# The layernorm statistics tail of an attention stage, moved behind the next slab's scores and shifted from VectorE to ScalarE

## The chip, the cores and the metric

One Trainium2 chip, 8 cores, each with its own 4096 tokens; no communication between them. The metric is the device time in microseconds of the slowest core. Engines: TensorE (PE), VectorE (DVE), ScalarE (ACT), GpSimd (POOL), SyncE (SP).

## The reference

Local attention over three neighbours, then a mixture of eight experts, each followed by a residual and a layernorm without weights:

```python
def _layernorm(x, axis=-1, eps=1e-5):
    m = jnp.mean(x, axis=axis, keepdims=True)
    v = jnp.var(x, axis=axis, keepdims=True)
    return (x - m) / jnp.sqrt(v + eps)
# x: (4, 8192, 1024), 16 heads of 64
xp = x @ Wp.T + bp
q = (xp @ Wq.T + bq) * scale; k = xp @ Wk.T + bk; v = xp @ Wv.T + bv
attn = softmax over the tokens s-1, s, s+1 of q . k
x = _layernorm(x + (attn-weighted v) @ Wo.T + bo)
# top 2 of 8 experts by sigmoid router, square(relu(x @ W1)) @ W2
x = _layernorm(x + ffn(x))
```

## The kernel before

All tensors of the attention stage are feature-major: 128 features on the partitions, 8 chunks of them (`dc`), 512 tokens along the free axis. A slab is 512 tokens; a core has 8 slabs. The weights Wp and Wq, Wk, Wv are multiplied together first. The feed-forward stage follows after a barrier of all engines (L691 to L699); it reads the normalised slabs back from HBM.

The order of the work is written out by hand: each `seg_` function appends instructions to the lists of the five engines, and every engine runs its own list strictly in order. The loop at L672 emits for each slab s:

1. `seg_scores(s)`: 24 products q times k on DVE into six slots (`pslots`, three per chunk), 32 matmuls on PE that sum them by head into `ps_s0` and `ps_s2`
2. `seg_softmax_a(s)`: two exponentials on ACT (L454, L456), their sum on DVE (L459)
3. `seg_ln1_tail(s-1)`: PE broadcasts the inverse deviation and the scaled mean from `stb` to 128 partitions (L623, L627), ACT copies both out of PSUM (L638, L640), DVE normalises the 8 chunks with 16 instructions, SP stores the slab
4. `seg_softmax_b(s)`: Ln and Exp on ACT (L466, L468), two weight products on DVE
5. `seg_qkv(s+1)`: 384 matmuls in 48 groups over two banks, each evicted by ACT (L407)
6. `seg_wsum(s)`, `seg_wo(s)`: weighted sum of v, output projection (64 matmuls), residual on DVE
7. `seg_ln1_stats_mm(s)`: sums and sums of squares over the features, by matmuls with a column of ones into `ps_s1` and `ps_st`, with the squares from DVE
8. `seg_xt(s+2)`: four x tiles and a halo of two tokens, loaded by POOL one after the other, transposed by PE (L340, L364), copied by ACT (L348, L372)
9. `seg_ln1_stats_tail(s)`: on one partition of 512 tokens, DVE scales sum and sum of squares, squares the mean and subtracts (L594 to L600), ACT does Ln and Exp for the inverse deviation (L605, L607), DVE multiplies it by the mean and casts both to bf16 in `stb` (L610 to L614)

Ahead of the loop stand `seg_xt(0)`, `seg_qkv(0)`, `seg_xt(1)`. The slabs 6 and 7 have no item 8, slab 7 has no item 5, and after the loop `seg_ln1_tail(7)` remains. A `drain` is put between two instructions of one engine that touch the same tensor.

Of the kernel before, what the change touches and what calls it, by code (L numbers as in the profile page):

```python
# [9 lines left out]
AF = mybir.ActivationFunctionType  # L10
# [3 lines left out]
D = 1024  # L14
# [80 lines left out]
def _h(ap):  # L95
    return ap.tensor if hasattr(ap, "tensor") else ap


def build_program(T):
    assert T % SLAB == 0  # L100
    NSLAB = T // SLAB
# [37 lines left out]
    s_pe = semh("s_pe")  # L139
    s_dve = semh("s_dve")  # L140
    s_act = semh("s_act")
# [3 lines left out]
    p = _Prog(block)  # L145
# [64 lines left out]
    for xi, (wxt_h, c_sb, cb_sb, scale) in enumerate(  # L210
# [4 lines left out]
        for dc in range(NCH):  # L215
            for jg in range(2):
# [3 lines left out]
                for kc in range(NCH):  # L220
# [5 lines left out]
                             inc=(s_pe if kc == NCH - 1 else None))  # L226
# [5 lines left out]
                          reads=[_h(role.t)], writes=[_h(c_sb)], inc=s_act)  # L232
                role.consumed(s_act, va)
        for jc in range(NCH):
            psfb.wait_writer(p)
            p.wait("tensor", s_ld, base_ld)
            for kc in range(NCH):
# [5 lines left out]
                         inc=(s_pe if kc == NCH - 1 else None))  # L243
# [5 lines left out]
                      reads=[_h(psfb.t)], writes=[_h(cb_sb)], inc=s_dve)  # L249
            psfb.consumed(s_dve, va)  # L250
        if xi < 2:
# [32 lines left out]
    stn = psb("stn", [1, 3 * 512], F32)  # L284
    stb = psb("stb", [1, 1024], BF16)
# [5 lines left out]
    ps_s = [_PsumRole(pst("ps_s0", [128, 512], F32)),  # L291
            _PsumRole(pst("ps_s1", [128, 512], F32)),
            _PsumRole(pst("ps_s2", [128, 512], F32))]
    ps_st = _PsumRole(pst("ps_st", [128, 512], F32))
# [7 lines left out]
    sn = lambda i: stn[:, i * 512:(i + 1) * 512]  # L302
# [10 lines left out]
    g_lnact = 0  # L313
# [6 lines left out]
    SS = {}  # L320
# [129 lines left out]
    def seg_softmax_a(s):  # L450
        p.wait("scalar", s_pe, SS[("scores", s)])
        p.wait("scalar", s_act, g_exp)
        p.wait("scalar", s_pe, g_mb)
        p.do("scalar", lambda En: En.activation(sm(0), ps_s[0].t[0:NH, :], AF.Exp),  # L454
             reads=[_h(ps_s[0].t)], writes=[_h(smt)], inc=s_act)
        v_e = p.do("scalar", lambda En: En.activation(sm(1), ps_s[2].t[0:NH, :], AF.Exp),  # L456
                   reads=[_h(ps_s[2].t)], writes=[_h(smt)], inc=s_act)
        p.wait("vector", s_act, v_e)
        v_sm = p.do("vector", lambda En: En.scalar_tensor_tensor(sm(2), sm(0), 1.0, sm(1), ALU.add, ALU.add),  # L459
                    reads=[_h(smt)], writes=[_h(smt)], inc=s_dve)  # L460
        SS[("v_sm", s)] = v_sm
        return v_e
# [125 lines left out]
        SS[("v2s", s)] = v2s  # L588

    def seg_ln1_stats_tail(s):  # L590
        p.wait("vector", s_pe, SS[("v2s", s)])
        p.wait("vector", s_act, g_lnact)
        p.wait("vector", s_pe, SS.get("v_mb", 0))
        p.do("vector", lambda En: En.tensor_scalar_mul(sn(0), ps_s[1].t[0:1, :], 1.0 / D),  # L594
             reads=[_h(ps_s[1].t)], writes=[_h(stn)], inc=s_dve)
        p.do("vector", lambda En: En.tensor_scalar_mul(sn(1), ps_st.t[0:1, :], 1.0 / D),
             reads=[_h(ps_st.t)], writes=[_h(stn)], inc=s_dve)
        p.do("vector", lambda En: En.tensor_mul(sn(2), sn(0), sn(0)),
             reads=[_h(stn)], writes=[_h(stn)], inc=s_dve)
        v_var = p.do("vector", lambda En: En.tensor_sub(sn(1), sn(1), sn(2)),  # L600
                     reads=[_h(stn)], writes=[_h(stn)], inc=s_dve)
        ps_s[1].consumed(s_dve, v_var)
        ps_st.consumed(s_dve, v_var)
        p.wait("scalar", s_dve, v_var)
        p.do("scalar", lambda En: En.activation(sn(2), sn(1), AF.Ln, bias=LN_EPS),  # L605
             reads=[_h(stn)], writes=[_h(stn)], inc=s_act)
        v_rs = p.do("scalar", lambda En: En.activation(sn(1), sn(2), AF.Exp, scale=-0.5),  # L607
                    reads=[_h(stn)], writes=[_h(stn)], inc=s_act)
        p.wait("vector", s_act, v_rs)
        p.do("vector", lambda En: En.tensor_mul(sn(2), sn(0), sn(1)),  # L610
             reads=[_h(stn)], writes=[_h(stn)], inc=s_dve)
        p.do("vector", lambda En: En.tensor_copy(stb[:, 0:512], sn(1)),
             reads=[_h(stn)], writes=[_h(stb)], inc=s_dve)
        v_stb = p.do("vector", lambda En: En.tensor_copy(stb[:, 512:1024], sn(2)),  # L614
                     reads=[_h(stn)], writes=[_h(stb)], inc=s_dve)
        SS[("v_stb", s)] = v_stb
        return v_rs

    def seg_ln1_tail(s):
        par = s % 2  # L620
        p.wait("tensor", s_dve, SS[("v_stb", s)])
        ps_s[1].wait_writer(p)
        p.do("tensor", lambda En: En.matmul(ps_s[1].t[:], onescol[0:1, :],  # L623
                                            stb[0:1, 0:512], start=True, stop=True),
             inc=s_pe)
        ps_st.wait_writer(p)
        v_mb = p.do("tensor", lambda En: En.matmul(ps_st.t[:], onescol[0:1, :],  # L627
                                                   stb[0:1, 512:1024], start=True, stop=True),
                    inc=s_pe)
        SS["v_mb"] = v_mb  # L630
        p.wait("scalar", s_pe, v_mb)
        sbp = pslots[2]
        mbp = pslots[3]
        for sl in (2, 3):
            if pslot_guard[sl] is not None:
                p.wait("scalar", *pslot_guard[sl])
                pslot_guard[sl] = None
        p.do("scalar", lambda En: En.copy(sbp, ps_s[1].t[:]),  # L638
             reads=[_h(ps_s[1].t)], writes=[pslot_t[2]], inc=s_act)
        v_bb = p.do("scalar", lambda En: En.copy(mbp, ps_st.t[:]),  # L640
                    reads=[_h(ps_st.t)], writes=[pslot_t[3]], inc=s_act)
        ps_s[1].consumed(s_act, v_bb)
        ps_st.consumed(s_act, v_bb)
        pslot_guard[2] = (s_act, v_bb)
        pslot_guard[3] = (s_act, v_bb)
        p.wait("vector", s_act, v_bb)
        if rstg_free[par] is not None:
            p.wait("vector", *rstg_free[par])
        for dc in range(NCH):
            t0n = pslots[dc % 2]  # L650
            p.do("vector", lambda En, o=t0n, r=r1c(s, dc):
                 En.tensor_mul(o, r, sbp),
                 reads=[_h(q_sb), pslot_t[2]], writes=[pslot_t[dc % 2]], inc=s_dve)
            p.do("vector",
                 lambda En, o=r1n_stg[:, par * NCH * SLAB + dc * SLAB: par * NCH * SLAB + (dc + 1) * SLAB],
                 a=t0n:
                 En.tensor_sub(o, a, mbp),
                 reads=[pslot_t[dc % 2], pslot_t[3]], writes=[_h(r1n_stg)], inc=s_dve)
        g_r1n[par] = s_dve.n
        p.wait("sync", s_hw, s_hw.n)  # L660
        p.wait("sync", s_dve, s_dve.n)
        p.do("sync",
             lambda En, o=r1n_hbm.rearrange("p (c t) -> p c t", t=T)[:, :, s * SLAB:(s + 1) * SLAB],
             i_=r1n_stg[:, par * NCH * SLAB:(par + 1) * NCH * SLAB].rearrange("p (c t) -> p c t", t=SLAB):
             En.dma_start(out=o, in_=i_),
             inc=s_hw, inc_by=16)
        rstg_free[par] = (s_hw, s_hw.n)
# [4 lines left out]
    for s in range(NSLAB):  # L672
        seg_scores(s)
        v_e = seg_softmax_a(s)
        g_exp = v_e
        if s >= 1:
            seg_ln1_tail(s - 1)
        seg_softmax_b(s)
        if s + 1 < NSLAB:
            seg_qkv(s + 1)  # L680
        seg_wsum(s)
        seg_wo(s)
        seg_ln1_stats_mm(s)
        if s + 2 < NSLAB:
            seg_xt(s + 2)
        v_rs = seg_ln1_stats_tail(s)
        g_lnact = v_rs
        g_mb = s_pe.n
    seg_ln1_tail(NSLAB - 1)

    p.wait("gpsimd", s_pe, s_pe.n)  # L691
# [332 lines left out]
    for Hh in range(NPASS):  # L1024
# [5 lines left out]
        for e in range(E):  # L1030
            for tt in range(NTT):
# [13 lines left out]
                for hdc in range(NCH):  # L1045
                    role = ps_hh[hdc % 2]
                    role.wait_writer(p)
                    for kc in range(NCH):
# [6 lines left out]
                                 inc=(s_pe if kc == NCH - 1 else None))  # L1055
# [3 lines left out]
                    if t1_free[hdc % 2] is not None:  # L1059
                        p.wait("scalar", *t1_free[hdc % 2])  # L1060
                    va = p.do("scalar", lambda En, o=t1, i_=role.t: En.activation(o, i_[:], AF.Relu),  # L1061
                              reads=[_h(role.t)], writes=[_h(t1u)], inc=s_act)
# [4 lines left out]
                         reads=[_h(t1u), _h(gbank.t)], writes=[_h(t1u)], inc=s_dve)  # L1067
# [3 lines left out]
                              reads=[_h(t1u)], writes=[_h(a_sb)], inc=s_dve)  # L1071
# [114 lines left out]
```

How the kernel before makes its waits and increments, by code:

```python
    def wait(self, eng, sem, val):  # L39
        if val <= 0:
            return
        self.ops[eng].append(lambda E, s=sem, v=val: E.wait_ge(s.h, v))
# [10 lines left out]
    def do(self, eng, fn, reads=(), writes=(), inc=None, inc_by=1):  # L53
        self._maybe_drain(eng, tuple(reads), tuple(writes))
        if inc is None:
            self.ops[eng].append(lambda E, f=fn: f(E))
        else:
            inc.n += inc_by
            self.ops[eng].append(lambda E, f=fn, s=inc, k=inc_by: f(E).then_inc(s.h, k))
        for h in writes:
            self.dirty[eng].add(id(h))
        for h in reads:
            self.read[eng].add(id(h))
        return inc.n if inc is not None else None
```

## Time and profile before

| | us |
|---|---|
| runs | 3509.01 and 3692.1, median 3600.56 |
| profiled execution | 3511.26 |
| its span on the slowest core (core 4) | 3509.7 |
| spans of the 8 cores | 3500.3 to 3509.7 |
| PE busy | 2886.5 (82%) |
| DVE busy | 1524.8 (43%) |
| ACT busy | 766.8 (22%) |
| attention stage | about 200 to 1162 |

Times in the rows are microseconds from the start of the span, on core 4. A row of the timeline gives start, duration, engine, line, operation and tiles, and in square brackets how long the engine had been idle before it and what released it. PEclk is the clock granted to TensorE as a share of its full 2.4 GHz.

### The profile page before, as it was taken

The numbers are of one execution on the slowest core, as the hardware profiler recorded it, in microseconds if no ns is written. First come the engines' busy times: TensorE is split into PE (matmuls) and PEld (weight loads), VectorE is DVE, ScalarE is ACT, GpSimd is POOL, SyncE is SP. The second block draws the span as 40 slices with busy tenths as digits, with TensorE's granted clock in tenths as the row PEclk, the third lists the DMA queues.
The fourth block names the chain that finished last, engine by engine and source line by source line (L and its number), as shares of the span: only waits on it lengthen the run. The fifth ranks groups of instructions, "written<-read, shape, count | busy, mean of one in ns | idle before, by whom it ended". The sixth has DMA issues, their size and how long they took to land.

```text
span 3509.7 us, 45369 instructions; the slowest of 8 cores (3500.3 to 3509.7 us)
## 1 busy us (share of the span) xinstructions
PE 2886.5 (82%) x13904; PEld 1333.9 (38%) x13904; DVE 1524.8 (43%) x2930; ACT 766.8 (22%) x1347; POOL 89.5 (3%) x127
## 2 busy tenths in 40 slices
PE   3577778887786499899779899968989987999984
PEld 1254434443442144344324344423434432444431
DVE  0002353435346344444554444455444455444444
ACT  1134334433442111111111111121111111111111
POOL 1000000000000000000000000000000000000000
PEclk9788878887887699999869999968999987899995
DMA  3410100010000543334315424423325241353511
GB/s 51 72 19 13 25 13 19 20 25 15 17 13 13 108 73 68 60 65 79 66 48 96 72 49 87 73 57 83 62 48 97 49 72 49 73 91 54 90 31 48
DMA packets 95063, 189.84 MB, mean 54 GB/s; under 512 B 3640, under 2 KB 11832, under 8 KB 94832
## 3 DMA queue, kind: packets, MB, share of 16 engines
q0 software_dynamic: 77744, 153.38, 25.8%
q1 hardware_dynamic: 17088, 33.56, 2.8%
q8 instruction: 123, 2.02, 0.2%
q14 instruction: 108, 0.88, 0.1%
HBM read 315.05 MB, written 25.17 MB: 97 GB/s over the span
## 4 chain that ended last, share of the span: by engine, by line
PE 56%; DMA 24%; DVE 7%; issue 6%; ACT 4%; DVEq 2%; ACTq 1%; POOLq 0%; POOL 0%; SPq 0%
PE ps_y L880 18%; PE ps_h L1054 15%; DMA w2e<-w 11%; PE ps_mm L401 10%; DMA w1e<-w 8%; PE ps_mm L551 3%; PE ps_f L225 3%; DMA xbt<-xs 2%; DVEq L49 2%; PE ps_b L994 2%; DVE otok L1003 1%; PE ps_s L445 1%; DVE y_acc L912 1%; ACT wbe L503 1%; ACT ln2scr L918 1%
## 5 line engine op out<-in xcount | busy, mean ns | idle before, releaser
L880 PE MATMUL ps_y<-a_sb,w2e 128*128 128x512 bf16 x4096 | 912.3, 384 | 41.0 <-DMA w2e<-w 26.3
L1054 PE MATMUL ps_h<-r1n_ps,w1e 128*128 128x512 bf16 x4096 | 908.5, 383 | 20.5 <-DMA w1e<-w 20.4
L1061 ACT ACTIVATE t1u<-ps_h 128x512 bf16<-128x512 f32 x512 | 305.7, 597 | 1587.9 <-PE ps_h L1054 1574.1
L880 PEld LDWEIGHTS ps_y<-a_sb,w2e 128*128 128x128 bf16 x4096 | 402.6, 99 | 545.5 <-issue 81.7
L1054 PEld LDWEIGHTS ps_h<-r1n_ps,w1e 128*128 128x128 bf16 x4096 | 398.9, 99 | 516.0 <-issue 55.4
L892 DVE TENSOR_TENSOR y_acc<-y_acc,ps_y 128x512 f32<-128x512 f32 x448 | 307.7, 687 | 447.1 <-PE ps_y L880 445.8
L1066 DVE TENSOR_TENSOR t1u<-t1u,ps_gb 128x512 bf16<-128x512 bf16 x256 | 175.9, 687 | 221.0 <-ACT t1u L1061 220.3
L1066 DVE TENSOR_TENSOR t1u<-t1u,ps_b 128x512 bf16<-128x512 bf16 x256 | 175.9, 687 | 189.0 <-ACT t1u L1061 188.5
L1070 DVE TENSOR_TENSOR a_sb<-t1u 128x512 bf16<-128x512 bf16 x512 | 217.5, 425 | 48.2 <-issue 1.3
L994 PE MATMUL ps_b<-id,y_acc 128*128 128x128 f32 x256 | 110.0, 433 | 72.9 <-DVE otok L1003 51.1
L551 PE MATMUL ps_mm<-k_sb,wot_sb 128*128 128x512 bf16 x512 | 139.3, 438 | 30.7 <-DVE pscr L522 24.2
L225 PE MATMUL ps_f<-wxt_sb,wp_sb 128*128 128x512 bf16 x384 | 90.4, 401 | 81.8 <-DMA wxt_sb<-wqt 47.9
L519 DVE TENSOR_TENSOR pscr<-wbe,v_sb 128x512 bf16<-128x512 bf16 x64 | 26.8, 418 | 264.2 <-ACT wbe L503 264.2
L1003 DVE TENSOR_SCALAR otok<-ps_b,mrs 128x128 f32<-128x128 f32 x256 | 104.9, 410 | 72.7 <-PE ps_b L994 57.5
L401 PE MATMUL ps_mm<-x_fm,ckt 128*128 128x257 bf16 x1024 | 121.5, 279 | 14.6 <-ACT k_sb L407 14.0
L401 PE MATMUL ps_mm<-x_fm,cvt 128*128 128x257 bf16 x1024 | 116.9, 273 | 0.5 <-ACT v_sb L407 0.3
L401 PE MATMUL ps_mm<-x_fm,cqt 128*128 128x257 bf16 x1024 | 116.6, 273 | 0.3 <-ACT q_sb L407 0.3
L401 PEld LDWEIGHTS ps_mm<-x_fm,ckt 128*128 128x128 bf16 x1024 | 94.4, 99 | 42.4 <-issue 19.5
L923 PE MATMUL ps_b<-ln2scr,onesv 128*1 128x512 bf16 x64 | 36.8, 575 | 79.5 <-ACT ln2scr L918 79.5
L401 PEld LDWEIGHTS ps_mm<-x_fm,cvt 128*128 128x128 bf16 x1024 | 91.6, 97 | 24.5 <-issue 1.3
L401 PEld LDWEIGHTS ps_mm<-x_fm,cqt 128*128 128x128 bf16 x1024 | 91.5, 97 | 24.1 <-issue 0.5
L551 PEld LDWEIGHTS ps_mm<-k_sb,wot_sb 128*128 128x128 bf16 x512 | 55.3, 108 | 114.9 <-issue 69.2
(151 smaller groups left out, 1701.0 us busy)
## 6 DMA issues: line engine op xcount, KB each, us to landing
w1e<-w POOLq DMA_DIRECT2D x32, 2048.0 KB, 14.3
w2e<-w POOLq DMA_DIRECT2D x32, 2048.0 KB, 14.8
out<-otok SPq DMA_DIRECT2D x32, 512.0 KB, 4.4
xbt<-xs POOLq DMA_DIRECT2D x32, 256.0 KB, 3.8
r1n_hbm<-r1n_stg SPq DMA_DIRECT2D x8, 1024.0 KB, 5.2
r1n_ps<-r1n_hbm SPq DMA_DIRECT2D x4, 2048.0 KB, 12.5
wp_sb<-wp POOLq DMA_DIRECT2D x1, 2048.0 KB, 16.7
wxt_sb<-wqt POOLq DMA_DIRECT2D x1, 2048.0 KB, 17.2
```

Source lines behind the costliest of these rows:

```text
L49: self.ops[eng].append(lambda E: E.drain())
L225: En.matmul(o[:], l, r, start=a, stop=b),
L401: En.matmul(o[:, 0:w_], l, r, start=a, stop=b),
L551: En.matmul(o[:], l, r, start=a, stop=b),
L880: En.matmul(o[:], l, r, start=a, stop=b),
L892: va = p.do("vector", lambda En, o=ydst, i_=role.t: En.tensor_add(o, o, i_[:]), reads=[_h(role.t), _h(y_acc)], writes=[_h(y_acc)], inc=s_dve)
L994: En.transpose(o[:, 0:128], src, id32[:]),
L1003: En.tensor_scalar(o, i_[:, 0:128], m, s_, ALU.subtract, ALU.mult),
L1054: En.matmul(o[:], l, r, start=a, stop=b),
L1061: va = p.do("scalar", lambda En, o=t1, i_=role.t: En.activation(o, i_[:], AF.Relu), reads=[_h(role.t)], writes=[_h(t1u)], inc=s_act)
L1066: p.do("vector", lambda En, o=u, a=t1, gb_=gbank.t: En.tensor_mul(o, a, gb_[:]), reads=[_h(t1u), _h(gbank.t)], writes=[_h(t1u)], inc=s_dve)
L1070: a=u, b=t1: En.tensor_mul(o, a, b),
```

## The change

`seg_ln1_stats_tail(s)` is no longer emitted at the end of iteration s, but in iteration s+1 after `seg_softmax_a(s+1)` and ahead of `seg_ln1_tail(s)`; that of the last slab follows the loop. Within it, the two scalings and the square of the mean go from DVE to ACT (Identity with a scale, Square), and so do the two casts into `stb`. The subtraction and the multiplication stay on DVE. The waits follow: PE waits for ACT's counter ahead of the broadcast, the statistics banks are released by ACT.

```diff
     def seg_ln1_stats_tail(s):
-        p.wait("vector", s_pe, SS[("v2s", s)])
-        p.wait("vector", s_act, g_lnact)
-        p.wait("vector", s_pe, SS.get("v_mb", 0))
-        p.do("vector", lambda En: En.tensor_scalar_mul(sn(0), ps_s[1].t[0:1, :], 1.0 / D),
-             reads=[_h(ps_s[1].t)], writes=[_h(stn)], inc=s_dve)
-        p.do("vector", lambda En: En.tensor_scalar_mul(sn(1), ps_st.t[0:1, :], 1.0 / D),
-             reads=[_h(ps_st.t)], writes=[_h(stn)], inc=s_dve)
-        p.do("vector", lambda En: En.tensor_mul(sn(2), sn(0), sn(0)),
-             reads=[_h(stn)], writes=[_h(stn)], inc=s_dve)
+        p.wait("scalar", s_pe, SS[("v2s", s)])
+        p.wait("scalar", s_dve, g_lnact)
+        p.wait("scalar", s_pe, SS.get("v_mb", 0))
+        p.do("scalar", lambda En: En.activation(sn(0), ps_s[1].t[0:1, :], AF.Identity,
+                                                scale=1.0 / D),
+             reads=[_h(ps_s[1].t)], writes=[_h(stn)], inc=s_act)
+        va1 = p.do("scalar", lambda En: En.activation(sn(1), ps_st.t[0:1, :], AF.Identity,
+                                                      scale=1.0 / D),
+                   reads=[_h(ps_st.t)], writes=[_h(stn)], inc=s_act)
+        v_sq = p.do("scalar", lambda En: En.activation(sn(2), sn(0), AF.Square),
+                    reads=[_h(stn)], writes=[_h(stn)], inc=s_act)
+        ps_s[1].consumed(s_act, va1)
+        ps_st.consumed(s_act, va1)
+        p.wait("vector", s_act, v_sq)
         v_var = p.do("vector", lambda En: En.tensor_sub(sn(1), sn(1), sn(2)),
                      reads=[_h(stn)], writes=[_h(stn)], inc=s_dve)
-        ps_s[1].consumed(s_dve, v_var)
-        ps_st.consumed(s_dve, v_var)
...
         p.wait("vector", s_act, v_rs)
-        p.do("vector", lambda En: En.tensor_mul(sn(2), sn(0), sn(1)),
-             reads=[_h(stn)], writes=[_h(stn)], inc=s_dve)
-        p.do("vector", lambda En: En.tensor_copy(stb[:, 0:512], sn(1)),
-             reads=[_h(stn)], writes=[_h(stb)], inc=s_dve)
-        v_stb = p.do("vector", lambda En: En.tensor_copy(stb[:, 512:1024], sn(2)),
-                     reads=[_h(stn)], writes=[_h(stb)], inc=s_dve)
+        v_mm2 = p.do("vector", lambda En: En.tensor_mul(sn(2), sn(0), sn(1)),
+                     reads=[_h(stn)], writes=[_h(stn)], inc=s_dve)
+        p.do("scalar", lambda En: En.copy(stb[:, 0:512], sn(1)),
+             reads=[_h(stn)], writes=[_h(stb)], inc=s_act)
+        p.wait("scalar", s_dve, v_mm2)
+        v_stb = p.do("scalar", lambda En: En.copy(stb[:, 512:1024], sn(2)),
+                     reads=[_h(stn)], writes=[_h(stb)], inc=s_act)
         SS[("v_stb", s)] = v_stb
-        return v_rs
+        return v_mm2

     def seg_ln1_tail(s):
         par = s % 2
-        p.wait("tensor", s_dve, SS[("v_stb", s)])
+        p.wait("tensor", s_act, SS[("v_stb", s)])
...
         if s >= 1:
+            g_lnact = seg_ln1_stats_tail(s - 1)
             seg_ln1_tail(s - 1)
         seg_softmax_b(s)
...
         seg_ln1_stats_mm(s)
         if s + 2 < NSLAB:
             seg_xt(s + 2)
-        v_rs = seg_ln1_stats_tail(s)
-        g_lnact = v_rs
         g_mb = s_pe.n
+    g_lnact = seg_ln1_stats_tail(NSLAB - 1)
     seg_ln1_tail(NSLAB - 1)
```

## Rows read from the trace of the kernel before

**Rows 1.** Windows by stage: busy us (instructions) of PE, PEld, DVE, ACT, POOL; PEclk, DMA share, GB/s

```profile
200.00:1162.00 962.00, 732.02 (x4488) 406.76 (x4488) 380.10 (x848) 365.78 (x681) 20.16 (x39) 0.82 0.09 18
```

**Rows 2.** Waits, 250 to 1300: who waited for whom, us, times, longest

```profile
DVE stn L610 <- ACT stn L607: 71.2, 8, 12.9
...
PE ps_s L445 <- DVE pscr L434: 30.2, 7, 7.0
```

**Rows 3.** Timeline of slab 3, from the last transposes to the first scores

```profile
617.78 0.34 PE L364 MATMUL ps_tb<-idb,xh 2*128 2x2 bf16 x8 [1.39 <-DMA xh<-xs]
...
619.83 0.68 DVE L610 TENSOR_TENSOR stn<-stn 1x512 f32<-1x512 f32 x1 [11.12 <-ACT stn L607]
...
622.00 0.59 PE L445 MATMUL ps_s<-pscr,spk_sb 128*16 128x512 bf16 x1 [3.87 <-DVE pscr L434]
```

**Rows 4.** Timeline of slab 3, from the end of the scores into qkv

```profile
632.83 0.38 PE L445 MATMUL ps_s<-sqscr,spkn_sb 128*16 128x512 bf16 x1
...
633.14 0.39 PE L623 MATMUL ps_s<-stb,onescol 1*128 1x512 bf16 x1
...
634.09 0.59 ACT L456 ACTIVATE smt<-ps_s 16x512 bf16<-16x512 f32 x1
634.58 0.56 ACT L638 CAST pscr<-ps_s 128x512 bf16<-128x512 f32 x1
...
637.53 0.71 PE L401 MATMUL ps_mm<-x_fm,ckt 128*128 128x257 bf16 x5 [1.92 <-ACT k_sb L407]
```

**Rows 5.** Timeline, last transposes and last scores matmul of slab 0, then slab 1

```profile
274.27 0.34 PE L364 MATMUL ps_tb<-idb,xh 2*128 2x2 bf16 x8 [2.06 <-DMA xh<-xs]
...
284.86 0.38 PE L445 MATMUL ps_s<-sqscr,spkn_sb 128*16 128x512 bf16 x1
...
387.10 0.34 PE L364 MATMUL ps_tb<-idb,xh 2*128 2x2 bf16 x8 [2.32 <-DMA xh<-xs]
...
401.58 0.38 PE L445 MATMUL ps_s<-sqscr,spkn_sb 128*16 128x512 bf16 x1
```

**Rows 6.** Timeline of slab 7, the first scores matmul

```profile
1073.73 0.58 PE L445 MATMUL ps_s<-pscr,spk_sb 128*16 128x512 bf16 x1 [7.00 <-DVE pscr L434]
```

**Rows 7.** Groups by line: count | busy us, mean ns | idle us before, releaser

```profile
L607 ACT ACTIVATE stn<-stn 1x512 f32<-1x512 f32 x8 | 5.0, 628 | 0.6
L454 ACT ACTIVATE smt<-ps_s 16x512 bf16<-16x512 f32 x8 | 4.7, 587 | 104.2 <-PE ps_s L445 104.2
L600 DVE TENSOR_TENSOR stn<-stn 1x512 f32<-1x512 f32 x8 | 5.4, 680 | 0.7
L348 ACT ACT_TABLE_LOAD x1 | 1.3, 1283 | 13.1 <-PE ps_tb L340 13.1
```

**Rows 8.** Windows around two starts of PE from idleness, slab 3 and slab 0

```profile
622.00:626.00 4.00, 4.00 (x10) 1.20 (x11) 3.58 (x10) 0.00 (x0) 0.53 (x1) 0.50 0.39 61
...
216.00:220.00 4.00, 4.00 (x20) 2.78 (x21) 0.00 (x0) 0.81 (x2) 0.54 (x1) 0.50 0.45 68
222.00:224.00 2.00, 2.00 (x20) 1.61 (x19) 0.00 (x0) 0.95 (x2) 0.00 (x0) 1.00 0.81 118
```

**Rows 9.** Timeline, the broadcast after the last slab

```profile
1145.30 0.58 PE L623 MATMUL ps_s<-stb,onescol 1*128 1x512 bf16 x1 [6.76 <-DVE stb L614]
```

**Rows 10.** Waits, 250 to 1300: the x tiles

```profile
POOL xbt L160 <- PE ps_tb L340: 626.5, 7, 99.5
...
PE ps_tb L340 <- DMA xbt<-xs: 54.7, 14, 5.5
```

**Rows 11.** Chain that ended last, two slabs' output projection

```profile
354.39 12.62 PE ps_mm L551 x57
...
584.66 15.06 PE ps_mm L551 x57
```

**Rows 12.** Windows after two issues of an x tile by POOL

```profile
608.10:609.60 1.50, 0.00 (x0) 0.00 (x0) 0.61 (x1) 0.11 (x1) 0.00 (x0) 1.00 0.87 130
...
624.40:625.90 1.50, 1.50 (x5) 0.42 (x4) 1.27 (x5) 0.00 (x0) 0.00 (x0) 0.50 0.84 146
```

## Prediction, made before the changed kernel ran

> **What bounds the kernel now.** I read the page first, then the windows by stage, then the waits of the attention stage, then the timeline of single slabs. The windows show the attention stage from 200 to 1162 us, with TensorE (PE) busy 732 of 962 us at a mean granted clock of 0.82 [rows 1]. The reader is to see that the change can move only these 962 us: the rest of the span, projection folding and feed-forward, runs none of the edited lines. In the waits [rows 2] two things matter. PE waits for the first product of `seg_scores` 7 times, 30.2 us in all, the longest 7.0. VectorE (DVE) waits 8 times, 71.2 us in all, for the exponential of `seg_ln1_stats_tail` (L607) before it may go on.
>
> The timeline of slab 3 shows why [rows 3]. The last transposes of `seg_xt` start at 617.78. Only behind them in ScalarE's (ACT) queue stand the Ln and Exp of the statistics tail, then DVE's multiply at 619.83 and two casts, and only then the first product; PE starts the scores at 622.00 after 3.87 us of idleness. In six slabs this gap is 3.87, in the last, where no `seg_xt` stands between, 7.0: 6 x 3.87 + 7.0 = 30.2, the sum in the waits.
>
> The end of the scores in the same slab [rows 4]: the last scores matmul ends at 632.83 + 0.38 = 633.21, PE goes straight on with the two broadcast matmuls of `seg_ln1_tail` (the first at 633.14) and with `seg_qkv`; that stalls once, 1.92 us, until 637.53, because ACT first does softmax_a, the two copies of the tail and softmax_b. From there `seg_qkv` is PE's own work.
>
> **Part 1: the tail no longer stands ahead of the scores.** Its ACT and DVE instructions leave the place between `seg_xt` and the products. DVE can make products right after the last square, up to the six slots, while PE is still waiting for x tiles. The trace has this case already: scores(0), which follows seg_xt(1) without a tail [rows 5]. There it takes from the start of the last transposes (274.27) to the end of the last scores matmul (284.86 + 0.38 = 285.24) 10.97 us. With the tail it takes 401.58 + 0.38 - 387.10 = 14.86 in slab 1 and 633.21 - 617.78 = 15.43 in slab 3; the six slabs lie between these, I take 15.15. Gain 15.15 - 10.97 = 4.2 each, 6 x 4.2 = 25. It isn't the whole wait plus more, because 18 of the 24 products still have to be made at DVE's pace behind slots that PE frees. In the last slab the gap of 7.00 ends with the tail [rows 6], and products follow the squares directly: 7.0. Together 32.0. Bounds: 3.87 x 6 + 7.0 = 30.2 if only the waits go, 6 x 4.5 + 7.0 = 34.0 by slab 3's figure.
>
> **Part 2: the tail stands between the scores and the broadcast.** It is emitted after softmax_a(s), so nine ACT and two DVE instructions come between the last scores matmul and `stb`, and PE has nothing else in its queue: behind the broadcast stands all of `seg_qkv`. Prices [rows 7]: ACT on 1x512 in SBUF 0.628, with 0.08 between two that share a tile, so 0.70 a step; ACT from PSUM 0.587; DVE 0.68. From the timelines: ACT to DVE 0.15, DVE to ACT 0.09, ACT to PE about 0.12. Square and Identity on one partition are not in this trace; I price them as the Ln and the Exp beside them (bounds 0.49 and 0.71 a step, the spacings of 634.09 to 634.58 and of Ln to Exp). Worked out in slab 3's own times:
> - second softmax exponential 634.09 [rows 4]; Identity 634.58, Identity 635.25, Square 635.95 to 636.58
> - DVE subtract 636.73 to 637.41; Ln 637.50; Exp 638.21 to 638.84
> - DVE multiply 638.99 to 639.67, under it the first copy of ACT; second copy 639.76 to 640.35
> - broadcast matmuls from 640.48, against 633.14 today [rows 4]: 7.3 later.
>
> The clock enters here. After PE's one unbroken gap of 7.00 us, in slab 7, the first scores matmul lasts 0.58 us [rows 6] against 0.38 at full clock [rows 5], and the stretch in which slab 3's scores start has a granted clock of 0.50, that is 1.2 GHz [rows 8]; a gap of 7.3 us will do the same. So the two broadcast matmuls last 0.43 + 0.63 and end at 641.54, and ACT's copies start at 641.73 against 634.58, 7.15 later. The first qkv groups run cold: 20 matmuls took 4.00 us at 0.50 and 2.00 us at 1.00 in slab 0 [rows 8], so the first 16 end at 644.8. That is just when ACT frees the bank (641.73 + 2.95, today's 637.53 - 634.58, = 644.68). The cold start thus takes the place of today's stall of 1.92 and is nearly hidden; were ACT faster, it would cost 1.7. PE resumes at 644.8 against 637.53: 7.3 later. In slab 0 the clock came back 4 to 6 us after PE started; here 0 to 1.7 us of half speed remain, 0 to 0.8 lost, I take 0.4. So 7.7 a slab, 6 x 7.7 = 46.2. In the last slab no qkv follows; softmax_b and the weights move by the 7.15 of ACT, and PE is cold there today as well: 7.2. Together 53.4. Bounds: with steps of 0.49 for Identity and Square 6.9 a slab and no lost clock, 48; with 8.1, 56.
>
> The Trainium skill, TensorE: Matmul & The Clock Gate, section "HAM oscillation", says that a wait in every tile of a loop throws PE back to its low clock and that each tile then starts cold; by that rule alone, charging the half of 4 us at half speed, a slab would cost 2 us more, 12 in all. The trace agrees that the clock falls, but its stall of 1.92 covers the start.
>
> **Part 3: the rest.** DVE loses four reads and two casts a slab; its 16 normalising instructions start 7 us later but lie beside 41 us of qkv, and their next reader, the q eviction, comes two thirds through it: nothing. If that cover were gone, 8 us, as in the last slab, where they stand ahead of the weights today too. SP's store waits for the same instructions and nobody for it. The tail after the last slab: today 6.76 from PE's last statistics to the broadcast [rows 9]; by the steps above 6.1: -0.6.
>
> **Sum.** 53.4 - 32.0 - 0.6 = +20.8 us on the profiled execution's 3511.3 us (its span 3509.7 and 1.6 around it): 3532. The two runs shown, 3509.0 and 3692.1, have a median of 3600.6; the profile sits at the lower one, and I predict on that scale. 0.6% is within the 2% that a measurement of this kernel can tell.
>
> **Rivals.**
> - Absorption (faster). If x tiles arrived at times of their own, the 7.7 would be taken up in `seg_xt`, where PE waits 54.7 us for them [rows 10], and only the gain would stay: 3511.3 - 32.0 + 7.2 - 0.6 = 3486. It decides once 3.5 of the 7.7 are absorbed. Against it: POOL's loads themselves wait for PE's transposes, 626.5 us in 7 waits [rows 10], so they move along. 4%.
> - The clock in `seg_wo`. Its 57 matmuls take 12.62 us in one slab and about 15 in another [rows 11], by whether PE kept its clock. New timing could bring six slabs to the fast side: 6 x 2.4 = 14 less, 3518. Nothing speaks for it but chance. 8%.
> - A table switch. Square is not in today's program. The one load of the stage took 1.283 us [rows 7]; if Square needed another set, two loads in each of 8 tails lie on the path: 20.5 more, 3553. The Trainium skill, ScalarE: Activation LUTs, section "Table sets", says that cheap functions fill every set but doesn't list square among them; with its full cost of a switch, 2.66 us, it would be an estimated 3575. Today Copy, Identity, Exp and Ln share one set without reloading. 8%.
> - x loads held up by products. Six products now run while POOL issues the next x tile. If the issue waited for all of them, 1.5 us a slab: 3541. Against it: the load issued at 622.97 amid products moved its data as the one at 606.70 without any, 0.84 and 0.87 busy in the stretch from 1.5 us on [rows 12]. The Trainium skill, SBUF — State Buffer, section "SBUF: two separate sides", has the rule that a DVE operation can lock GpSimd out of writing descriptors; this row does not show it for these products. 5%.
> - Cold qkv. If the clock stayed at half through the whole of qkv, 384 x 0.1 = 38 us a slab, 3760. It passes 2% (+70 us) from 8 us a slab. Slab 0 speaks against [rows 8]. 3%.
>
> The forecast itself 72%, with its own range 3518 to 3545. The range for all, 3510 to 3558, takes in the clock of wo and the table switch. Faster by over 2% 0.02, within 0.94, slower 0.04.
>
> **What would show it.** Right: the wait of 3.87 ahead of the scores gone, DVE products under the x waits; a new wait of about 7 us of PE for ACT's `stb` ahead of the broadcast in 7 slabs; granted clock 0.50 at qkv's start; the slab period longer by 3.5. Wrong: a broadcast less than 5 us after the scores, scores ending less than 3 us earlier, table loads in the stage, or a qkv that is still cold at its tenth group.

## The result: 0.5% slower, and the profile after

| | before | after |
|---|---|---|
| median of all runs, us | 3536.56 (12 runs) | 3534.39 (13 runs) |
| lowest, us | 3509.01 | 3526.73 |
| profiled execution, us | 3511.26 | 3531.19 |
| ratio to before | | 1.0052, 95% interval 1.0039 to 1.0065 |

Some executions of either kernel are disturbed on one die and take up to 10% longer, so that the median of before was 3600.56 over its first two runs and is 3536.56 over twelve; the ratios in this document leave such executions out, and they alone say which kernel is faster.

The waits of the changed kernel from 250 to 1300 us, on core 0, the slowest core of its profiled execution (who waited for whom: us, times, longest), to be set beside [rows 2]:

```profile
DVE pscr L434 <- PE ps_s L445: 101.2, 19, 22.4
...
PE ps_s L627 <- ACT stb L618: 58.0, 8, 7.4
...
DVE stn L613 <- ACT stn L610: 13.0, 8, 1.6
```

VectorE waits 13.0 us for the exponential where it was 71.2. It now makes its first six products under the x waits and then waits for TensorE to free a slot, 101.2 us in 19 times (25.0 in 7 before). TensorE's 30.2 us for the first products are gone (0.2 us are left). In their place TensorE waits 58.0 us for the broadcast's operand: seven times 7.4 and once 6.2 at the very end, where it was 6.76 [rows 9]. The timeline of slab 3, core 0 (start, us, instruction, idle before), to be set beside [rows 3] and [rows 4]:

```profile
621.13 0.35 PE L364 MATMUL ps_tb<-idb,xh 2*128 2x2 bf16 x8 [2.08 <-DMA xh<-xs]
621.49 0.59 PE L445 MATMUL ps_s<-pscr,spk_sb 128*16 128x512 bf16 x1
...
631.93 0.38 PE L445 MATMUL ps_s<-sqscr,spkn_sb 128*16 128x512 bf16 x1
632.51 0.59 ACT L454 ACTIVATE smt<-ps_s 16x512 bf16<-16x512 f32 x1 [10.73 <-PE ps_s L445]
...
633.67 0.57 ACT L594 ACTIVATE stn<-ps_s 1x512 f32<-1x512 f32 x1
...
634.99 0.63 ACT L600 ACTIVATE stn<-stn 1x512 f32<-1x512 f32 x1
635.72 0.68 DVE L605 TENSOR_TENSOR stn<-stn 1x512 f32<-1x512 f32 x1 [1.17 <-ACT stn L600]
636.53 0.63 ACT L608 ACTIVATE stn<-stn 1x512 f32<-1x512 f32 x1 [0.92 <-DVE stn L605]
...
638.83 0.62 ACT L618 CAST stb<-stn 1x512 bf16<-1x512 f32 x1 [0.27 <-DVE stn L613]
639.70 0.58 PE L627 MATMUL ps_s<-stb,onescol 1*128 1x512 bf16 x1 [7.39 <-ACT stb L618]
...
640.64 16.25 PE L401 MATMUL ps_mm<-x_fm,ckt 128*128 128x257 bf16 x128
```

The first scores matmul starts right behind the transposes. From the start of the transposes to the end of the scores are 632.31 - 621.13 = 11.2 us, where it was 15.4 [rows 3, 4]. Then the ScalarE chain stands bare, 7.39 us, and `seg_qkv` runs its first 128 matmuls without the old stop of 1.92 us. The windows of the same slab (busy us and instructions of PE, PEld, DVE, ACT, POOL; PEclk, DMA share, GB/s) show the clock, mostly at 0.50 for the first 4 us and at 1.00 from 644 us on:

```profile
640.00:644.00 4.00, 4.00 (x20) 2.29 (x18) 1.40 (x4) 2.68 (x5) 0.00 (x0) 0.57 0.00 0
644.00:646.00 2.00, 2.00 (x19) 1.68 (x18) 1.63 (x5) 1.00 (x3) 0.00 (x0) 1.00 0.00 0
646.00:650.00 4.00, 4.00 (x38) 3.20 (x37) 2.99 (x8) 2.30 (x5) 0.00 (x0) 1.00 0.01 2
```

To add the parts up, TensorE's timeline is cut into sections, from the first instruction of one kind of work to the first of the next. Each section is summed over the slabs and the mean of the eight cores taken (us, one profiled execution of each kernel; in brackets how many slabs have the section). "Halo transposes" are those of the two extra tokens that end each `seg_xt`:

| section | before | after | after - before |
|---|---|---|---|
| halo transposes to end of scores (7 slabs) | 101.4 | 78.3 | -23.1 |
| last statistics to end of scores (slab 7) | 17.6 | 10.7 | -6.9 |
| end of scores to broadcast (7; slab 0 to qkv) | -0.5 | 51.8 | +52.3 |
| broadcast to qkv (6) | 3.2 | 5.6 | +2.4 |
| qkv to weighted sum (7) | 320.6 | 318.3 | -2.3 |
| weighted sum (8) | 141.1 | 141.3 | +0.2 |
| output projection (8) | 157.9 | 154.8 | -3.1 |
| statistics (6), x tiles (6) | 104.1 | 103.2 | -0.9 |
| slab 7, broadcast to weighted sum | 12.5 | 11.9 | -0.6 |
| last broadcast | 6.8 | 6.2 | -0.6 |
| whole, first halo transposes to last broadcast | 933.1 | 950.8 | +17.7 |

(The whole is longer than the sum of the rows: it also holds slab 0's qkv, the x tiles of slab 1 and the last slab's statistics, about 69 us in both kernels. The differences of the rows add up to 17.4.)

### The profile page after: what moved, and what is told of

It reads as the page before. It is cut to its first block, busy times and chain, and to the rows that moved or that the text cites. A ratio compares the mean times of both kernels' runs of the same rounds, so it can differ in the third digit from the quotient of the medians.

```text
span 3529.6 us, 45190 instructions; the slowest of 8 cores (3473.7 to 3529.6 us)
## 1 busy us (share of the span) xinstructions
PE 2877.7 (82%) x13709; PEld 1339.2 (38%) x13904; DVE 1503.7 (43%) x2890; ACT 791.0 (22%) x1387; POOL 89.4 (3%) x127
## 4 chain that ended last, share of the span: by engine, by line
PE 56%; DMA 23%; DVE 7%; issue 6%; ACT 4%; DVEq 2%; ACTq 1%; POOLq 0%; POOL 0%; SPq 0%
PE ps_y L884 18%; PE ps_h L1058 15%; DMA w2e<-w 11%; PE ps_mm L401 10%; DMA w1e<-w 8%; PE ps_mm L551 3%; PE ps_f L225 3%; DMA xbt<-xs 2%; PE ps_b L998 2%; DVEq L49 2%; DVE otok L1007 2%; PE ps_s L445 1%; DVE y_acc L916 1%; ACT wbe L503 1%; ACT ln2scr L922 1%
## 5 line engine op out<-in xcount | busy, mean ns | idle before, releaser
L884 PE MATMUL ps_y<-a_sb,w2e 128*128 128x512 bf16 x4011 | 902.0, 383 | 46.3 <-DMA w2e<-w 26.6
L1058 PE MATMUL ps_h<-r1n_ps,w1e 128*128 128x512 bf16 x4010 | 905.0, 384 | 26.6 <-DMA w1e<-w 20.9
L884 PEld LDWEIGHTS ps_y<-a_sb,w2e 128*128 128x128 bf16 x4096 | 402.1, 99 | 541.6 <-issue 76.1
L1074 DVE TENSOR_TENSOR a_sb<-t1u 128x512 bf16<-128x512 bf16 x512 | 217.7, 425 | 47.7 <-issue 0.9
L434 DVE TENSOR_TENSOR pscr<-q_sb,k_sb 128x512 bf16<-128x512 bf16 x128 | 51.7, 423 | 161.4 <-PE ps_s L445 101.2
## 6 DMA issues: line engine op xcount, KB each, us to landing
wxt_sb<-wqt POOLq DMA_DIRECT2D x1, 2048.0 KB, 18.2
```

What stands on the lines that cost most here:

```text
L884: En.matmul(o[:], l, r, start=a, stop=b),
L1058: En.matmul(o[:], l, r, start=a, stop=b),
L1074: a=u, b=t1: En.tensor_mul(o, a, b),
```

## The experiments

The theory that the prediction rests on, Q in the expectations: a place of the tail costs what of it TensorE waits for, whole, and the two places add up. Rivals: E, that the move to ScalarE carries the cost; M, that only the place matters; A, that the x waits or the clock absorb a part; C, that a cold clock is paid in full at the start of qkv; X, that an earlier tail holds up the x tiles. W is a later theory, on the clock in the output projection. The extra matmuls of `warm`, `wo_warm` and the `_w7` kernels write a transposition bank that is free at that time, and nobody reads them.

### The place alone: `move_only`

The loop of the changed kernel, with the function of the kernel before (against the changed kernel):

```diff
-        p.do("scalar", lambda En: En.activation(sn(0), ps_s[1].t[0:1, :], AF.Identity, ...
+        p.do("vector", lambda En: En.tensor_scalar_mul(sn(0), ps_s[1].t[0:1, :], 1.0 / D),
... (all of seg_ln1_stats_tail as before)
```

> Only the place of the tail is changed as in the changed kernel; its instructions stay on VectorE as before. Theory Q (both places are waits of TensorE, whole and in series: gain about 3.9 us ahead of the scores, loss the length of the chain behind them): the chain is longer here, because the four VectorE instructions stand behind the sum of the exponentials and four steps of 0.77 us, the multiply and two casts follow: about 8.9 us from the last scores matmul to the broadcast against 7.4 with ScalarE. So about 1.5 us a slab more than the changed kernel, 10 us in all: 3542, ratio to before about 1.0085. Rival E (it is the move to ScalarE that costs, since VectorE casts in 0.415 us and ScalarE in 0.62): the gap is shorter than 7.4 and the time is below the changed kernel's 3531, near 3520, ratio 1.003 or less.

Ratio to before 1.0047 (1.0024 to 1.0070). The timeline of slab 3, core 0:

```profile
643.15 0.58 PE L623 MATMUL ps_s<-stb,onescol 1*128 1x512 bf16 x1 [8.69 <-DVE stb L614]
```

The wait is 8.69 against 7.39, close to the 8.9 expected, so E is wrong about the chain: at this place ScalarE is the faster engine for it. Yet the time did not follow: a ratio of 1.0085 was expected. From first halo to last broadcast it is 953.6 us, only 2.8 more than the changed kernel. The sections say where the 9.0 us of longer waits ahead of the broadcasts (60.8 instead of 51.8) and 3.6 us more in qkv (321.9 instead of 318.3) went: the output projection, which no edit touches, is 144.3 instead of 154.8 us. That was the open question for the later runs.

### The engines alone: `act_only`

The function of the changed kernel, at the old place (against the changed kernel):

```diff
         if s >= 1:
-            g_lnact = seg_ln1_stats_tail(s - 1)
             seg_ln1_tail(s - 1)
...
         if s + 2 < NSLAB:
             seg_xt(s + 2)
+        v_rs = seg_ln1_stats_tail(s)
+        g_lnact = v_rs
         g_mb = s_pe.n
-    g_lnact = seg_ln1_stats_tail(NSLAB - 1)
```

> Only the engines are changed as in the changed kernel; the tail stays ahead of the next scores. Theory Q: the three ScalarE instructions stand behind the x copies, where before VectorE had done this work under the x waits, so products start about 2.0 us later in six slabs (gap 5.9 instead of 3.87), about 1 us earlier in the last, and the end gains 0.6: +10 to +11 us on before, 3522, ratio 1.003. Rival E (the engine move carries the whole loss of 18 to 20 us): 3530, ratio 1.005 or more. Rival M (only the place matters): ratio 1.000.

Ratio 1.0013 (0.9984 to 1.0041), which alone tells little. The trace, slab 3, core 0:

```profile
612.23 0.17 ACT L372 COPY x_fm<-ps_tb 128x16 bf16<-128x16 bf16 x1 [1.37 <-PE ps_tb L364]
612.42 0.59 ACT L594 ACTIVATE stn<-ps_s 1x512 f32<-1x512 f32 x1
...
617.95 0.59 PE L445 MATMUL ps_s<-pscr,spk_sb 128*16 128x512 bf16 x1 [5.85 <-DVE pscr L434]
```

The gap is 5.85, expected 5.9. The section from halo to end of scores is 112.7, +11.3; slab 7 gains 0.8 and the end 0.6. The projection is 4.6 shorter without an edit to it, qkv and the x tiles together 1.6, so that the whole stage is +3.0 instead of +10. M, that only the place matters, is wrong: the same engines cost 11 us where the x copies stand ahead of them in ScalarE's queue.

### A longer chain: `dose`

The changed kernel with the Square done three times:

```diff
-        v_sq = p.do("scalar", lambda En: En.activation(sn(2), sn(0), AF.Square),
+        for _rep in range(3):
+            v_sq = p.do("scalar", lambda En: En.activation(sn(2), sn(0), AF.Square),
```

> The changed kernel with the Square done three times over instead of once (same result): two more ScalarE steps of 0.70 us in every tail. Theory Q: the chain stands bare on the path in all eight places: 8 x 2 x 0.70 = +11.3 us on the changed kernel, 3542, ratio to before 1.0085; the wait of TensorE for stb grows from 7.4 to 8.8. Rival A (absorption: the x waits or the clock take up part of a longer chain): less than +5, ratio below 1.0067.

Ratio 1.0067 (1.0047 to 1.0087). Slab 3, core 0:

```profile
643.42 0.58 PE L628 MATMUL ps_s<-stb,onescol 1*128 1x512 bf16 x1 [8.81 <-ACT stb L619]
```

7.39 + 2 x 0.71 = 8.81: each step of ScalarE reaches TensorE whole. Over the slabs the waits are 61.7 instead of 51.8 and the last 7.7 instead of 6.2, together +11.4 as expected. The whole stage is only +7.6, with qkv at 321.6 instead of 318.3 and the projection at 148.1 instead of 154.8. Of A, the part on the x waits is refuted: the x tiles take 76.1 against 76.3. The part on the clock is not: the ratio sits at A's bound of 1.0067, and whether the longer chain or chance made the projection 6.7 us shorter, this run can't say.

### A clock kept up: `warm`

The changed kernel with 28 matmuls of 512 columns ahead of the broadcast, into the bank of `ps_tb1`:

```diff
     def seg_ln1_tail(s):
         par = s % 2
+        if s < NSLAB - 1:
+            ps_tb[1].wait_writer(p)
+            for _w in range(28):
+                v_w = p.do("tensor",
...
+                           En.matmul(warm_ps, l, r, start=True, stop=True),
```

> The changed kernel with 28 matmuls of 512 columns whose result nobody reads, put into TensorE's queue ahead of the broadcast in the seven tails within the loop, about 6 us of work, so that its clock does not fall in the wait for stb. Theory Q as in the prediction (the cold start is nearly hidden behind ScalarE's four instructions ahead of the first eviction): the two broadcast matmuls are 0.4 us shorter and the residue of 0 to 0.8 goes: 0.8 to 1 us a slab, -5 to -6 us in all, ratio 1.0035. Rival C (a cold start costs in full, half of 4 to 5 us at half speed, 2 to 2.5 us a slab): -12 to -15 us, ratio 1.001. The granted clock at the start of qkv should be 1.00 in place of 0.50.

Ratio 1.0038 (0.9990 to 1.0085), inconclusive by itself. A window of slab 3, core 0:

```profile
640.00:644.00 4.00, 2.69 (x25) 2.06 (x23) 3.22 (x8) 2.67 (x6) 0.00 (x0) 1.00 0.00 0
```

and TensorE's timeline:

```profile
637.93 0.37 PE L636 MATMUL ps_s<-stb,onescol 1*128 1x512 bf16 x1 [1.25 <-ACT stb L619]
...
638.45 1.94 PE L402 MATMUL ps_mm<-x_fm,ckt 128*128 128x257 bf16 x16
641.70 0.49 PE L402 MATMUL ps_mm<-x_fm,ckt 128*128 128x257 bf16 x3 [1.31 <-ACT k_sb L408]
```

With the clock at 1.00 the first 16 matmuls of qkv are done early and TensorE stops again, 1.31 us, for ScalarE. So the cold start does take the place of a stall. Over cores 0 to 3 (on cores 4 and 5 of this execution three qkv took 52 to 53 us each) the broadcasts gain 2.5 us in all (5.6 to 3.1) and qkv 2.6 (317.9 to 315.3). Of the 2.6, 0.4 lie in the qkv of slab 1, ahead of which no broadcast stands, so that the warm start is worth 4.7 us: a little under the 5 to 6 that Q expected, and far from the 12 to 15 of C. In most slabs qkv takes about 45.0 us in both kernels; the gain is in the few in which the changed kernel takes 46.1 to 46.4. The stage as a whole is 938.7 against 950.6, 11.9 shorter, which by the total alone would look like C; 3.7 of that is in the x tiles, which C does not speak of, and no cause for it is known (last section).

### The clock of the output projection: `wo_warm`, `changed_w7`, `move_w7`

`wo_warm` is the changed kernel with five extra matmuls behind the three broadcasts of each chunk in `seg_wsum`; `changed_w7` and `move_w7` are the changed kernel and `move_only` with the same, but in slabs 0 to 6 alone:

```diff
                                En.matmul(ot[:], l, r, start=True, stop=True),
                                inc=s_pe)
+            ps_tb[1].wait_writer(p)
+            for _w in range(5):
+                v_w = p.do("tensor",
...
+                           En.matmul(warm_ps, l, r, start=True, stop=True),
```

> The changed kernel with five matmuls of 512 columns, whose result nobody reads, behind the three of each chunk of the weighted sum, where TensorE waits for ScalarE. In the traces so far the output projection takes 17.4 to 17.8 us when TensorE has its full clock at its start and 19 to 20.5 when not, and the sum over eight slabs differed between kernels (158 before, 155 changed, 144 with the tail moved alone), which hid up to 10 us of a difference. Theory W (the clock falls in the weighted sum because TensorE is little busy there, and which slabs are hit depends on timing): projection at 17.8 in all slabs but perhaps the last, sum 142 to 144, the weighted sum as long as before (141): -11 to -13 us on the changed kernel, 3519, ratio 1.0015. Rival: the extra matmuls lengthen the weighted sum (over 150 in all) and nothing is won.

Ratio 1.0028 (1.0008 to 1.0048). One stretch of the weighted sum of slab 2, core 0, in `wo_warm`:

```profile
560.00:572.00 12.00, 11.95 (x51) 3.84 (x50) 10.16 (x26) 9.05 (x17) 0.00 (x0) 1.00 0.01 2
```

and the same stretch of its slab 2 in the kernel before:

```profile
560.00:572.00 12.00, 8.32 (x15) 1.39 (x14) 10.16 (x26) 9.03 (x17) 0.00 (x0) 0.50 0.00 1
```

VectorE and ScalarE do the same in both; TensorE's 15 matmuls alone leave the clock at 0.50, 51 keep it at 1.00. The weighted sum takes 17.5 to 17.7 in the slabs 0 to 6 on this core (17.8 to 18.2 before), and the projections take 143.3 in sum instead of the changed kernel's 154.8 (eight cores). In slab 7 the extra matmuls begin at the low clock and are in the way, 28.9 us instead of 18.3. There the clock stays low in stretches in which TensorE is never idle:

```profile
1104.00:1108.00 4.00, 4.00 (x11) 0.94 (x10) 2.40 (x7) 2.04 (x4) 0.00 (x0) 0.50 0.01 2
```

So both W and its rival were half right, 11.5 us won and 10.3 lost; the stage is 7.4 us shorter than the changed kernel's, 4.7 of it in the x tiles. The next two kernels leave slab 7 alone.

One thing W has wrong is where the clock matters. Two projections of the kernel before, slabs 0 and 1 of core 0, timeline and windows:

```profile
347.53 12.61 PE L551 MATMUL ps_mm<-k_sb,wot_sb 128*128 128x512 bf16 x56 [0.80 <-DVE k_sb L531]
...
461.82 15.01 PE L551 MATMUL ps_mm<-k_sb,wot_sb 128*128 128x512 bf16 x56 [0.79 <-DVE k_sb L531]
```

```profile
344.00:346.00 2.00, 2.00 (x5) 0.73 (x5) 1.69 (x5) 0.58 (x1) 0.00 (x0) 0.50 0.00 0
348.00:352.00 4.00, 4.00 (x20) 1.81 (x20) 1.89 (x3) 0.00 (x0) 0.00 (x0) 1.00 0.00 0
...
458.00:462.00 4.00, 2.94 (x7) 0.92 (x7) 3.12 (x8) 0.88 (x2) 0.00 (x0) 0.50 0.00 2
462.00:466.00 4.00, 4.00 (x10) 1.47 (x10) 0.77 (x2) 0.00 (x0) 0.00 (x0) 0.50 0.00 0
```

They start at 343.97 and 458.27, both at 0.50, and run alike for 3.5 us (six matmuls, then a wait for VectorE). In the fast one the clock is at 1.00 when the dense part begins, in the slow one it is still at 0.50 some 4 us into it; that is the difference between 12.61 and 15.01 us. A full clock at the start is no safeguard: slab 6 of `changed_w7` on core 0 starts its projection at 1040.83 at 1.00, loses the clock inside it and takes 19.4 us:

```profile
1041.00:1045.00 4.00, 1.91 (x9) 0.64 (x8) 3.07 (x8) 0.83 (x2) 0.00 (x0) 1.00 0.00 0
1045.00:1049.00 4.00, 4.00 (x13) 1.56 (x13) 1.50 (x2) 0.00 (x0) 0.00 (x0) 0.59 0.00 0
```

What decides when the clock returns or falls is not shown by these runs.

> The changed kernel with five matmuls of 512 columns, whose result nobody reads, in each chunk of the weighted sum of the slabs 0 to 6. In the last slab, where wo_warm took 28.9 us for the weighted sum instead of 18, there are none. Theory W: the weighted sum is 17.6 in all slabs, projections near 17.8 in the slabs 1 to 6, so that this kernel and move_w7 can be compared without the chance of the projection's clock. From first halo to last broadcast 943 (wo_warm) less 11 for the last weighted sum plus 2 to 4 for its projection: 935 us; ratio to before 1.0000.

> The same addition in the kernel in which the tail is moved and stays on VectorE. Theory Q with W: its gap of 8.69 against 7.40 shows in full now, +9 us, and the start of qkv costs some 3 us more, as it did in the two traces (321.9 against 318.3): 947 us from first halo to last broadcast, 12 us more than changed_w7, ratio 1.0035. Rival E (the move to ScalarE gains nothing): the two kernels are equal within 3 us, as they were without the addition (954 and 951).

| | changed_w7 | move_w7 |
|---|---|---|
| ratio to before | 1.0008 (0.9998 to 1.0018) | 1.0035 (1.0021 to 1.0049) |
| end of scores to broadcast | 51.8 | 60.8 |
| qkv | 318.6 | 321.0 |
| weighted sum | 140.7 | 140.5 |
| output projection | 148.4 | 145.6 |
| first halo to last broadcast | 937.2 | 947.0 |

Expected were 935 and 947 us. The two now differ by 9.8 us, against 2.8 without the addition, the difference of their waits is 9.0, and the intervals of their ratios no longer overlap. That settles the open question: the move to ScalarE does save about 9 us behind the scores, and in the plain pair the clock of the projection had hidden it. Not all projections are at 17.8 (core 0 of `changed_w7` has 19.4 in three slabs), so 2 to 3 us of this chance are left in the comparison: `move_w7` has 2.8 less in the projection and 2.4 more in qkv.

### Neither wait: `early`, `best`, `best_warm`, `best_w7`

`early` is the kernel before with its tail one step earlier, ahead of the x tiles:

```diff
         seg_ln1_stats_mm(s)
+        v_rs = seg_ln1_stats_tail(s)
         if s + 2 < NSLAB:
             seg_xt(s + 2)
-        v_rs = seg_ln1_stats_tail(s)
```

> The kernel before, with the tail emitted between the statistics matmuls and the x tiles of slab s+2 instead of behind them (its instructions and engines as before). Theory Q (a tail costs what of it TensorE waits for): VectorE and ScalarE run it under the x waits, at the price of the first x copy starting some 4 us later, of which about 0.4 reaches the third x tile; products are ready when TensorE comes to the scores, and the broadcast follows the scores without a gap. So the gain of the change without its loss: 6 x 4 - 6 x 0.4 = 21 to 23 us less than before, 3489, ratio 0.994; the gap of 7.0 in the last slab stays. Rival X (the later x copies delay the x chain by the length of the tail, 4 us): no gain, ratio 1.000.

Ratio 0.9907 (0.9876 to 0.9938). The timeline of slab 2, core 0:

```profile
590.87 1.07 PE L340 MATMUL ps_tb<-idb,xbt 128*128 128x128 bf16 x16
...
595.51 2.07 ACT L348 COPY x_fm<-ps_tb 128x1024 bf16<-128x1024 bf16 x2
...
596.75 1.01 PE L340 MATMUL ps_tb<-idb,xbt 128*128 128x128 bf16 x8 [4.82 <-ACT x_fm L348]
...
597.38 1.78 DVE L434 TENSOR_TENSOR pscr<-q_sb,k_sb 128x512 bf16<-128x512 bf16 x4
...
600.49 1.01 PE L340 MATMUL ps_tb<-idb,xbt 128*128 128x128 bf16 x8 [2.72 <-DMA xbt<-xs]
```

The whole tail runs while the third x tile is on its way. The x copies start late, the third tile waits 4.82 for a copy instead of 4.01 for its data (the same slab before), and the fourth, which then waits 2.72 instead of 3.41, takes most of it back: the x tiles take 76.5 in all against 76.8. Scores 77.8 instead of 101.4, broadcast behind them without a gap (-0.5), the stage 906.0: -27.1 on before, -44.8 on the changed kernel. That is more than the 21 to 23 expected (ratio 0.994): 23.6 are the scores, 2.3 the unedited projection and 0.8 qkv. X is wrong.

For slab 7, which has no x tiles, `best` splits the tail: Identity, Identity, Square, Ln, Exp and the casts are on ScalarE, and `seg_scores` calls VectorE's two steps after the products of the second and the fourth chunk:

```diff
+        if s == NSLAB - 1:
+            seg_scores(s, {1: seg_tail_sub, 3: lambda: seg_tail_mul(NSLAB - 2)})
...
```

> As early, and in the last slab, which has no x tiles to hide behind, the tail is split: Identity, Identity, Square, Ln, Exp and the two casts on ScalarE, which is idle there, and VectorE's subtraction and multiplication between the products of the second and fourth chunk. Theory Q: of the gap of 7.0 there, 1.5 (two VectorE steps) stay: 5.5 us less than early, 3484, ratio 0.9925. Rival: the products wait for ScalarE at the hooks and half of it is lost, -2 to -3 against early.

Ratio 0.9908 (0.9877 to 0.9938), not to be told from `early`; in the trace slab 7 takes 12.0 from statistics to end of scores instead of 17.6, and the stage 898.9 instead of 906.0.

`best_warm` adds the matmuls of `wo_warm`, `best_w7` those of `changed_w7`:

```diff
+            for _w in range(5 if s < NSLAB - 1 else 0):
+                v_w = p.do("tensor",
...
+                           En.matmul(warm_ps, l, r, start=True, stop=True),
```

> best and wo_warm together. Theory: the two gains add up: best's 3484 less 12 to 14 for the projections, 3471, ratio 0.989. If TensorE's waits elsewhere take it up, no better than best.

> best with the same addition: 895 (best_warm) less 11 plus 2 to 4: 887 us from first halo to last broadcast, 9 us less than best_warm, 3468, ratio 0.986.

Ratios 0.9886 (0.9855 to 0.9917) and 0.9890 (0.9870 to 0.9911); stages of 895.4 and 886.6 us, expected 895 and 887. In the stage the parts add up; in the ratio the two can't be told apart, all four intervals overlap, and the 0.986 expected of `best_w7` lies outside its interval. What is shown is that all four beat both kernels: by 0.9 to 1.1% that of before.

## Why the prediction came out as it did

**The step that failed.** It is the base of the sum: "The two runs shown, 3509.0 and 3692.1, have a median of 3600.6; the profile sits at the lower one, and I predict on that scale." Set against the 3600.6 that was given as the time before, 3532 says 1.9% faster, while the argument says slower, and slower was measured: 1.0052 (1.0039 to 1.0065). Against the 3511.3 from whose rows it was worked out, 3532 is 1.0059, within that interval. A change of half a per cent has to be stated as a ratio to the run that the rows come from; one absolute figure beside a median of two runs 183 us apart states the opposite.

**The sum.** +20.8 us on the profiled execution before was predicted, +19.9 measured (3531.19 against 3511.26). That they lie so close is partly luck. The attention stage gives +17.7 of the 19.9, the other 2.2 arise where the prediction has no term. In the stage the gain was forecast 2.0 us too large and the loss 0.9, and -3.1 in the projection and some -1 in other sections without an edit had been put at nothing; the errors go both ways.

**Part 1, the gain.** 25 + 7.0 predicted, 23.1 + 6.9 measured. The mechanism was right; the term of a slab is 3.8 to 3.9 instead of 4.2, since the scores take 11.2 to 11.6 from the halo in most slabs and not the 10.97 of slab 0 [rows 5].

**Part 2, the loss.** The wait was summed to 7.3 and is 7.39, in every slab: Identity from PSUM 0.57 and 0.59, Square 0.63, as the nearest rows had it. The two casts are 0.62 each. 53.4 was predicted for all of it. Measured are 52.3 for the waits, 2.4 for the cold broadcasts, -1.6 for qkv in the six slabs with a broadcast ahead of it and -0.6 in slab 7: 52.5. (The other -0.6 or so of the table's -2.3 is in the qkv of slab 1, which takes about 46.0 or 47.7 in either kernel.) The step "here 0 to 1.7 us of half speed remain, 0 to 0.8 lost, I take 0.4" was wrong in size and sign: qkv is shorter than before by 0.3 a slab. `warm` confirms the reason given for the small cost, the swallowed stall.

**Part 3.** -0.6 at the end, measured -0.6. The later normalising instructions cost nothing: the weighted sum is unchanged.

**The rivals.** Absorption in the x waits: refuted, TensorE waits 53.8 us for x tiles after and 54.7 before, and all 11.4 us of `dose` appear as waits. Table switch: no load beyond the same three. The x loads beside products: the x tiles take 76.3 after and 76.8 before. Cold qkv: PEclk is 1.00 from 644 us on. The clock in `seg_wo` had been given 8% and "nothing speaks for it but chance"; it is real at -3.1 us here, and up to -13.6 in `move_only` (157.9 to 144.3). It had been priced well, 2.4 a slab, but treated as one more case, when it is a term with a spread that every comparison of this kernel carries. Its reason, "by whether PE kept its clock", is wrong: fast and slow projections both start at 0.50, and differ in when the clock comes back.

## What to carry to other kernels

Before moving a serial chain off one wait, write down what the bounding engine would do at the new place; here TensorE had nothing queued behind the scores, so a chain that had cost 3.9 us ahead of them cost 7.4 behind them, while some 9 us of waiting for x tiles a slab (4.0, 3.4 and 1.5 us in slab 2) stood free one line earlier in the same program. Compare sections of the trace, not only times: an untouched section moved by up to 13.6 us through its clock and hid a 9 us effect. And price a cold start by what waits beside it, not by its own length.

## What the runs showed of the hardware that was not expected

**The clock in a half-idle section is a matter of timing.** In the kernels without extra matmuls the output projection takes 17.4 to 18.1 us or 19.0 to 20.7. On all cores of these seven kernels both kinds start at a granted clock of 0.50. It is back at 1.00 after 2.3 to 3.9 us in the fast ones and after 7.0 to 9.5 us in the slow ones. Which slabs are fast changes from kernel to kernel: two of eight on core 0 of before, all but the first in `move_only`. In the weighted sum ahead of it the granted clock was 0.50 with TensorE busy 8.32 of 12 us at that clock, and 1.00 with the extra matmuls. Being busy did not bring it back in every case: in slab 7 of `wo_warm` TensorE was busy 4.00 of 4.00 us from 1104 to 1108 us, and the clock stayed at 0.50.

**Cores run in pairs.** In many executions of either kernel one pair of cores (0 and 1, 2 and 3, ...) is ahead of the rest, always both, one by some 50 to 80 us and the other by 25 less. The profiled one:

```profile
core 1: 3521.6 us, clock 0.872
core 2: 3473.7 us, clock 0.873
core 3: 3498.8 us, clock 0.873
core 4: 3528.2 us, clock 0.875
```

Their attention stages are as long as the others', but in the feed-forward stage TensorE waits for weights 15.1 + 1.0 us on core 2 and 1.1 + 20.8 on core 3, against 20.9 + 26.6 on core 0; and the two cores of such a pair end 25 us apart, the others 6 to 8. That the weight loads of a pair disturb each other unless the two cores are far enough apart fits this, but it was argued from these numbers and not tried.

**Open.** In the six kernels with extra matmuls the x tiles take 71.2 to 73.0 us in six slabs, in the other seven kernels, before and after among them, 76.0 to 76.8. The loads come 0.2 to 0.3 us sooner each. No edit touches the loads, though the extra matmuls write a bank that the x transposes use too, and no run tells why. Comparisons between a kernel with extra matmuls and one without carry these 4 to 5 us.
